# Attention scores on two half arrays of TensorE, even and odd heads side by side, six of nine products of parts, masks of 64 columns

## The reference

```python
q = (x @ Wq).reshape(bsz, seq_len, NH, HD).transpose(0, 2, 1, 3)
k = (x @ Wk).reshape(bsz, seq_len, KVH, HD).transpose(0, 2, 1, 3)
...
q = q * cos + rotate_half(q) * sin
k = k * cos + rotate_half(k) * sin
...
att = jnp.einsum('bhqd,bhkd->bhqk', q, k) * scale
att = jnp.where(causal, att, jnp.finfo(att.dtype).min)
att = jax.nn.softmax(att, axis=-1)
y = jnp.einsum('bhqk,bhkd->bhqd', att, v)
```

## Time and profile before

| | us |
|---|---|
| median of three runs | 1807.9 |
| the profiled execution | 1808.5 |
| its span, first to last instruction | 1806.8 |
| attention stage, from the first score product to the next stage | 232.4 to 855 |
| of it PE busy | 595.1 |
| of it DVE / ACT / POOL busy | 422.4 / 381.5 / 235.3 |
| PE clock granted in the stage | 0.96 of full speed |

### The profile page before, as it was taken

The page is one execution under the profiler, slowest core; times in us unless marked ns, Lnnn a source line. Parts: engine busy times, 40 slices in busy tenths (PEclk is TensorE's granted clock), DMA queues, the critical chain, the costliest instruction groups (busy, mean ns, idle before and its releaser), DMA issues. The chain is left out here.

```text
span 1806.8 us, 38981 instructions
## 1 busy us (share of the span) xinstructions
PE 1556.2 (86%) x11698; PEld 1092.2 (60%) x11698; DVE 1269.5 (70%) x3160; ACT 1156.7 (64%) x2439; POOL 771.7 (43%) x1202
## 2 busy tenths in 40 slices
PE   3999589999999999997799269999977834999998
PEld 1445245555555555553355159999964524999997
DVE  3787367777777777772786657787768766777776
ACT  3788316666666666665587347877847623788775
POOL 2587614334333444333343456655302203665540
PEclk9999759999999999998899579999989856999999
DMA  5022331111111111100011311111001100111110
GB/s 140 23 70 62 92 75 41 39 43 42 43 43 43 43 42 40 38 19 2 12 36 35 105 28 39 39 32 29 21 1 32 40 24 21 51 49 46 46 44 23
DMA packets 72828, 76.49 MB, mean 42 GB/s; under 512 B 13040, under 2 KB 61488, under 8 KB 72752
## 3 DMA queue, kind: packets, MB, share of 16 engines
q1 hardware_dynamic: 64560, 58.77, 11.2%
q0 software_dynamic: 8192, 16.79, 3.5%
HBM read 51.40 MB, written 24.12 MB: 42 GB/s over the span
## 5 line engine op out<-in xcount | busy, mean ns | idle before, releaser
L1024 DVE TENSOR_REDUCE at_negmax<-at_s_ps 128x2 f32<-128x1024 f32 (+3 forms) x384 | 393.2, 1045 | 170.3 <-PE at_s_ps L815 167.4
L936 ACT ACTIVATE at_p<-at_x_ps 128x512 f32<-128x512 f32 x640 | 353.5, 591 | 158.0 <-PE at_x_ps L825 151.2
L991 POOL TENSOR_SCALAR_AFFINE_SELECT at_p<-at_p 128x256 f32<-128x256 f32 (+1 forms) x448 | 190.8, 438 | 347.5 <-ACT at_p L936 347.5
L1248 POOL DMA_INDIRECT e_x_in<-xn,e_row_c x256 | 259.6, 1014 | 146.0 <-issue 85.0
L813 PE MATMUL at_s_ps<-at_kr,at_qr 72*128 72x512 bf16 (+3 forms) x1024 | 252.9, 312 | 23.2 <-DMA at_kr<-k_parts 20.7
L825 PE MATMUL at_x_ps<-at_qr,at_kr 74*128 74x512 bf16 (+3 forms) x1024 | 235.7, 305 | 22.6 <-ACT at_p L936 12.9
L1369 DVE TENSOR_TENSOR e_hid_lo<-e_hid,e_hid_hi 128x512 fp32r<-128x512 f32 x256 | 177.4, 694 | 83.2 <-ACT e_hid_hi L1333 74.5
L815 PE MATMUL at_s_ps<-maskb,identb 128*128 128x128 bf16 x1024 | 202.1, 225 | 0.0
L1332 ACT ACTIVATE e_hid<-e_h_ps 128x512 f32<-128x512 f32 x256 | 154.7, 604 | 42.1 <-PE e_h_ps L1274 37.4
L840 PE MATMUL at_o_ps<-at_p,at_va 128*32 128x512 f32 (+3 forms) x2048 | 155.5, 445 | 1.6 <-POOL at_p L991 1.6
L1274 PE MATMUL e_h_ps<-e_x_hi,w_hi 128*128 128x256 f32 x512 | 156.6, 306 | 0.0
(11 more groups left out here) (196 smaller groups left out, 3495.6 us busy)
## 6 DMA issues: line engine op xcount, KB each, us to landing
at_qr<-q_parts SPq DMA_DIRECT2D x192, 96.0 KB
k_parts<-m_kparts SPq DMA_DIRECT2D x48, 96.0 KB, 1.8
at_kr<-k_parts SPq DMA_DIRECT2D x64, 72.0 KB
xres<-in_x_dram SPq DMA_DIRECT2D x8, 512.0 KB, 7.6
xn<-m_n_xhat SPq DMA_DIRECT2D x16, 256.0 KB
e_x_in<-xn,e_row_c POOLq DMA_INDIRECT x256
xn<-sc_n_xhat SPq DMA_DIRECT2D x16, 256.0 KB
out_dram<-xres SPq DMA_DIRECT2D x16, 256.0 KB
```

The source lines that it names most:

```text
L936: a.activation(p_sb[g % 2][:, i, :], x_ps[i % 2][:], ACT.Exp, scale=SCALE).then_inc(x_read, 1)
L991: sel = gp.affine_select(out=part, in_=part, compare_op=ALU.is_ge, fill=0.0, base=0, pattern=[[0, n] for n in part.shape[1:-1]] + [[1, P]] ...
L1024: v.tensor_reduce(negmax[u][:, h0:h0 + len(heads), c], s_ps[k % 2][:, 0:len(heads) * pitch].rearrange("p (j w) -> p j w", w=pitch)[:, :, 0:w],
L1248: nc.gpsimd.indirect_dma_start(out=x_in[k][u][:], out_offset=None, in_=xn_dram, in_offset=bass.IndirectOffsetOnAxis(ap=row_c[k][:, u:u + 1 ...
```

## The change

The parts of q and k are paired six ways in place of nine: part 0 of k with parts 0, 1, 2 of q, part 1 with 0 and 1, part 2 with 0 (KEPT = 3, 2, 1), so KQ = 48 and KM = 50. The three smallest products of parts are left out. Partitions 0 to 63 now hold even heads and 64 to 127 odd heads, with the keys in both halves; qr shrinks to half its width. Score products of an even and an odd head are issued in pairs, one on the upper and one on the lower 64 rows of the array, into different banks. The mask, which had one product of 128 rows and 128 columns per head, has two of 64 rows and 64 columns per head (selb, maskb). The X tiles alternate between the halves (`i % 2`). max_rows moves from after X3 to after X2 and ahead of weigh, and ScalarE's copy of it from after the exponential of X4 to after that of X2. A group's loads are eight DMAs in place of four, and the maxima go to qr in two DMAs in place of one. One more constant of 256 columns is loaded and cast.

```diff
-KQ = PARTS * PARTS * HD
+KEPT = [PARTS - j for j in range(PARTS)]
+KFIRST = [sum(KEPT[:j]) for j in range(PARTS)]
+KQ = sum(KEPT) * HD
...
+HALF = P // 2
...
-        ("mhalf", W * C), ("wu", M * 4), ("wtop", M), ("maskf", P), ("gw", E), ("rowbase", 1),
+        ("mhalf", W * C), ("wu", M * 4), ("wtop", M), ("maskf", P), ("self", 2 * P), ("gw", E), ("rowbase", 1),
...
-        ("identb", [P, P], BF16), ("maskb", [P, P], BF16),
+        ("selb", [P, 2 * P], BF16), ("maskb", [P, P], BF16),
...
-                v.tensor_copy(h["identb"][:], h["ident"][:])
+                v.tensor_copy(h["selb"][:], h["self"][:])
...
-                            for copy in range(PARTS):
-                                sp.dma_start(k_dram[i * W + b].rearrange("(j c p) t -> c p j t", c=PARTS, p=KR)[copy],
-                                             rot["k"]["parts"][b * KR:(b + 1) * KR]).then_inc(parts_out[W], 16)
+                            rows = k_dram[i * W + b].rearrange("(x p) t -> p x t", p=KR)
+                            for j, copies in enumerate(KEPT):
+                                part = rot["k"]["parts"][b * KR:(b + 1) * KR, j, :]
+                                sp.dma_start(rows[:, KFIRST[j]:KFIRST[j] + copies, :],
+                                             part.unsqueeze(1).to_broadcast([KR, copies, T])).then_inc(parts_out[W], 16)
...
-          [[(2, 2 * i, 0), (2, 2 * i + 1, 256)] for i in range(GH // 2)]
+          [[(2, i, 0), (2, i + 2, 256)] for i in range(GH // 2)]
...
-S_TILES = [(3, (0, 1), 512), (3, (2, 3), 512), (2, (0, 1), 512), (2, (2, 3), 512), (1, (0, 1, 2, 3), 256), (0, (0, 1, 2, 3), 128)]
+S_TILES = [(3, (0, 1)), (3, (2, 3)), (2, (0, 1)), (2, (2, 3)), (1, (0, 1, 2, 3)), (0, (0, 1, 2, 3))]
...
-WEIGH_AT, ROWS_AT, MISC_AT = 2, 3, 7
+WEIGH_AT, MISC_AT = 2, 7
...
-        qr = [t(f"qr{u}", [P, NH * T], BF16) for u in range(2)]
+        qr = [t(f"qr{u}", [P, NH // 2 * T], BF16) for u in range(2)]
...
-                    q = q_dram[n].rearrange("(r h) t -> r h t", h=NH)
+                    q = q_dram[n].rearrange("(r g a s) t -> s g r a t", g=NKV, a=2, s=2)
...
-                    rows = PARTS * HD
-                    for j in range(PARTS):
-                        sp.dma_start(qr[u][j * rows:(j + 1) * rows, g * GH * T:(g + 1) * GH * T].rearrange("r (h t) -> r h t", h=GH),
-                                     q[:, g * GH:(g + 1) * GH, :]).then_inc(qk_in[u][g], 16)
-                    sp.dma_start(kr[u][0:KQ, g * T:(g + 1) * T], k[:, g, :]).then_inc(qk_in[u][g], 16)
+                    for half in range(2):
+                        for j, kept in enumerate(KEPT):
+                            at = half * HALF + KFIRST[j] * HD
+                            sp.dma_start(qr[u][at:at + kept * HD, g * 2 * T:(g + 1) * 2 * T].rearrange("r (a t) -> r a t", a=2),
+                                         q[half, g, 0:kept * HD]).then_inc(qk_in[u][g], 16)
+                        sp.dma_start(kr[u][half * HALF:half * HALF + KQ, g * T:(g + 1) * T], k[:, g, :]).then_inc(qk_in[u][g], 16)
...
-                    sp.dma_start(qr[u][KQ:KM, g * GH * T:(g + 1) * GH * T],
-                                 m_dram[u].rearrange("a r q -> a (r q)")[:, g * GH * T:(g + 1) * GH * T]).then_inc(m_in[u][g], 16)
+                    for half in range(2):
+                        sp.dma_start(qr[u][half * HALF + KQ:half * HALF + KM, g * 2 * T:(g + 1) * 2 * T].rearrange("a (x t) -> a x t", x=2),
+                                     m_dram[u].rearrange("a (g x s c) q -> s g a x (c q)", g=NKV, x=2, s=2)[half, g]).then_inc(m_in[u][g], 16)
...
-                def scores(n, u, r, g, k):
+                def scores(n, u, r, g, k, first):
...
-                        pe.wait_ge(qk_in[u][g], r * 64 + 64)
-                    c, heads, pitch = S_TILES[k]
+                        pe.wait_ge(qk_in[u][g], (r + 1) * 2 * (PARTS + 1) * 16)
+                    c, heads = S_TILES[k]
...
-                    for x, j in enumerate(heads):
-                        q0, at = (g * GH + j) * T + c * P, x * pitch
-                        pe.matmul(s_ps[k % 2][:, at:at + w], qr[u][0:KQ, q0:q0 + P], kr[u][0:KQ, g * T:g * T + w],
-                                  start=True, stop=False)
-                        mm = pe.matmul(s_ps[k % 2][:, at + w - P:at + w], h["identb"][:], h["maskb"][:], start=False, stop=True)
+                    for a in range(len(heads) // 2):
+
+                        pair = []
+                        for half in (first, 1 - first):
+                            rows = slice(half * HALF, half * HALF + KQ)
+                            q0 = (g * 2 + (heads[0] + 2 * a) // 2) * T + c * P
+                            pair.append((slice(half * HALF, (half + 1) * HALF), half * T + a * w))
+                            pe.matmul(s_ps[k % 2][:, half * T + a * w:half * T + (a + 1) * w], qr[u][rows, q0:q0 + P],
+                                      kr[u][rows, g * T:g * T + w], start=True, stop=False)
+                        for x in range(2):
+                            for rows, at in pair:
+                                at += w - P + x * HALF
+                                mm = pe.matmul(s_ps[k % 2][:, at:at + HALF], h["selb"][rows, x * P:(x + 1) * P],
+                                               h["maskb"][rows, x * HALF:(x + 1) * HALF], start=False, stop=x == 1)
...
-                        pe.wait_ge(m_in[u][g], r * 16 + 16)
+                        pe.wait_ge(m_in[u][g], (r + 1) * 2 * 16)
...
+                    rows = slice(i % 2 * HALF, i % 2 * HALF + KM)
...
-                        q0 = (g * GH + j) * T
-                        mm = pe.matmul(x_ps[i % 2][:, at:at + T - c * P], kr[u][0:KM, g * T + c * P:g * T + (c + 1) * P],
-                                       qr[u][0:KM, q0 + c * P:q0 + T], start=True, stop=True)
+                        q0 = (g * 2 + j // 2) * T
+                        mm = pe.matmul(x_ps[i % 2][:, at:at + T - c * P], kr[u][rows, g * T + c * P:g * T + (c + 1) * P],
+                                       qr[u][rows, q0 + c * P:q0 + T], start=True, stop=True)
...
-                                scores(*ahead, S_BEFORE[i])
+                                scores(*ahead, S_BEFORE[i], i % 2)
...
+                            if i == WEIGH_AT and ahead_rows is not None:
+                                max_rows(*ahead_rows, use(n, g, True))
...
-                            if i == ROWS_AT and ahead_rows is not None:
-                                max_rows(*ahead_rows, use(n, g, True))
...
-                            scores(*FIRST, g, k)
+                            scores(*FIRST, g, k, 0)
...
+                            if i == WEIGH_AT and ahead_rows is not None:
+                                copy_rows(ahead_rows[0], ahead_rows[3], use(n, g, True))
...
-                            if i == ROWS_AT + 1 and ahead_rows is not None:
-                                copy_rows(ahead_rows[0], ahead_rows[3], use(n, g, True))
...
-                    c, heads, pitch = S_TILES[k]
+                    c, heads = S_TILES[k]
...
-                    v.tensor_reduce(negmax[u][:, h0:h0 + len(heads), c],
-                                    s_ps[k % 2][:, 0:len(heads) * pitch].rearrange("p (j w) -> p j w", w=pitch)[:, :, 0:w],
-                                    AX.X, ALU.max, negate=True).then_inc(s_read, 1)
+                    scored = s_ps[k % 2][:].rearrange("p (s x) -> p s x", s=2)[:, :, 0:len(heads) // 2 * w]
+                    if len(heads) == 2:
+                        out = negmax[u][:, h0:h0 + 2, c]
+                    else:
+                        scored = scored.rearrange("p s (a w) -> p a s w", w=w)
+                        out = negmax[u][:, h0:h0 + GH, c].rearrange("p (a s) -> p a s", s=2)
+                    v.tensor_reduce(out, scored, AX.X, ALU.max, negate=True).then_inc(s_read, 1)
...
-        k_dram = dram("k_parts", [NB, PARTS * 96, T], BF16)
+        k_dram = dram("k_parts", [NB, KQ * NKV, T], BF16)
...
-    w["mask"] = np.where(at[None, :] > at[:, None], f32(MASKED), f32(0))
+    row, last = at % HALF, at % HALF == HALF - 1
+    later = np.where(row[:, None] < np.arange(HALF)[None, :], f32(MASKED), f32(0))
+    w["mask"] = np.concatenate([later, np.where(last[:, None], f32(MASKED), later)], 1)
+    same = (row[:, None] == np.arange(HALF)[None, :]).astype(f32)
+    none = np.zeros((P, HALF), f32)
+    w["self"] = np.concatenate([same, none, np.where(last[:, None], f32(1), none), np.where(last[:, None], f32(0), same)], 1)
```

## The result

The changed kernel takes 1810.35 us (median of 12 runs, 1808.26 to 1818.22), the kernel before 1808.15 in the same measurements (12 runs): a ratio of 1.0023, with a 95% interval of 1.0012 to 1.0034. That is no gain, at most 0.3% lost, where 1774 had been forecast. The profiled execution has a span of 1809.7 us against 1806.8.

A forecast was written before the change was run, and what follows sets the result against it. PE's instruction stream in the attention step was taken as the bound, with DVE and ACT not far behind. 1808.5 - 35.4 + 1 + 0.6 = 1774.7, set to 1774 us against the median; range 1748 to 1812.

The forecast's parts named there:

- What bounds the kernel: Attention stage: PE's stream sets the step, 35.74 of 36.98 us busy; DVE and ACT mostly wait for PE.
- The step: Attention steps with scores ahead: 0.6 us shorter each, 59 steps, 35.4 us in all (bounds 21 and 50).
- (a): Rival: short mask products are paced by their issue, four costing 0.23 us; steps 0.3 us longer, 1828 us; chance 0.08.
- (c): Rival: products on the two half arrays don't overlap here; 1808 to 1812 us, no change; chance 0.06.
- rival (d): X tiles on the other half overlap scores, misc passings free: 0.85 to 1 us a step, 1750; chance 0.08.
- max_rows: Row transpose in the attention step, now between X2 and weigh: keeps 0.11 us, its wait for the maxima adds nothing.
- The end of the stage: Last three attention steps: they have no scores and gain nothing.
- rival (b): PE's clock falls once in a step and returns with weigh: plus 24 + 2, 1834 us; chance 0.12.
- The start: Start of the attention stage, up to the first weigh: net plus 1 us, bounds minus 2 and plus 4.
- The 0.6 us for the constant of 256 columns: Constant adding 128 KB ahead of all compute: plus 0.6 us.

The follow-up runs named there:

- before_split: The kernel before with each mask product of 128 columns cut into two of 64, on the full array: 1838.5 us, ratio 1.0175.
- after_halfmask: The changed kernel with only the second of each head's two mask products, 16 instead of 32 a step: 1794.2 us, ratio 0.9932.
- before_six: The kernel before with six of nine products of parts, on the full array with 128-column masks, and nothing else: 2288.5 us, ratio 1.2656.

## Why the prediction was wrong

**What bounds the kernel** was read rightly: PE's stream in the step, with DVE and ACT waiting for it. Fewer masks, and the transpose taken off the way to weigh, shortened the step; idle products in PE's waiting for ACT did not lengthen it.

**The step** was right but for a small part. X5 comes 1.30 us after S2's start, X7 2.38 (forecast 1.30 and 2.37), X8 3.53, X2 5.68 and weigh 6.20 once the 0.5 us of project are taken off (3.48, 5.62, 6.1). The gain was 0.53 us and not 0.6, so 31 us in place of 35. Pairs ran side by side, and four masks took 0.06 us: rivals (a) and (c) did not come. That 1810 us lies where rival (c) had put the time is chance. X tiles on the other half did run beside score products, as rival (d) supposed (at 479.96 X1 and a product of S1 start 3 ns apart), but the step gained no more by it. The Trainium skill (TensorE: Matmul & The Clock Gate, Wait — 56ns, not 53.3ns?) gives about 62 ns for each matmul where hardware decoding is off; by an estimate from that figure four masks would take 0.25 us. The row from 500.91 to 500.97 decides against it here.

**max_rows** stood on the path between X2 and weigh at 0.11 us, and that was near: 0.48 us were forecast from X2 to weigh, 0.52 came. What had no term is the place that it left, behind weigh, where the waiting of X5 covered it. Put back there, in straight-line code, it saves 0.13 us a step.

**The code of the loop** is the step of the forecast that failed. The part on the change went through products, masks, loads and waits, and had no term for the fact that TensorE's loop grew from 1526 to 1782 recorded instructions. The five jumps, at no cost before, took 27.4 us: 17.1 of stops, and the rest in steps at a low clock behind them. before_split shows the stops without any half array, after_halfmask shows their absence with them. Nothing in the rows that I chose could price it, but the page's row of q8 and the times of its packets would have shown that the kernel before kept its loop loaded, which is the thing that could be lost.

**The end of the stage** was put down as no gain. It lost 5.9 us. Rows had it before them: the same steps brought the clock down once before (827.4 to 834.2). I took this as evidence on rival (b) within the steps and not on the place where it stood. That the clock falls was right in rival (b), but not where it put it: it fell at the jumps, in the two steps after the first weigh, and at the end, and in no other step of the loop.

**The start** was forecast 1 us later. The first weigh came 3.5 earlier. The loads began 1.3 us earlier than before and took 25.5 us, so the first maxima were stored at 252.35 and not 255; X began 3.4 us after that, where I had put 4.5; and from X0 to weigh it was 9.7 us, where I had 10.2. The two steps behind it gave 3.8 back. The 0.6 us for the constant of 256 columns had no row behind it and did not show: the stage began 1.3 us earlier than before.

That the last kernel stands at 1773.7 does not make the forecast right. It has no loop, merged masks, the transpose moved back and idle products: changes that the forecast did not speak of.

## What to carry to other kernels

Count the instructions of a loop on each engine before and after a change, and look whether the code queue is silent while the loop runs; if a change makes it speak in every pass, the jump has a price that no dependency shows. Here work was taken off the engine that is the bound, and its clock fell where it had not before; look for the stretches in which it now waits, and price them at the low clock, or fill exactly those. Fewer rows in a product are no gain by themselves: beside masks of 128 rows, products of 48 rows cost a passing each way, and the change avoided it by cutting both to halves.

## What the runs showed of the hardware

- A loop with 1526 recorded instructions on TensorE (1376 of them products and weight loads) stayed loaded, q8 silent behind the first pass, at both places tried. Loops of 1654 and 1782 (1504 and 1632 products and weight loads) did not, at any place tried. PE stood still 3.2 to 3.9 us at the jump, in two kernels once more for 1.3 to 2.8. With 256 of the 1782 being counter increments it did stay loaded. What exactly is counted, and how the place shapes the stop, is open.
- Straight-line code of over 11,000 TensorE instructions was fetched without a stop, by 64 to 72 packets in the whole kernel. The changed kernel's steps were 0.1 us longer in it than inside the loop; from 300 to 800 us X tiles waited 54.2 us for ACT in place of 42.1. Why was not settled.
- Passing from a product of 48 rows to one of 128 and back cost 0.1 us each way at the full clock; from 72 rows to 128 nothing that can be seen.
- In the changed kernel's steps the two products of S0, S2, S3 and S5 on two half arrays started 3 to 6 ns apart, and four masks of 64 columns on the halves took 0.06 us. In S4, and mostly in S1, the two started 0.14 to 0.22 us apart: one ran beside the X tile ahead, the other stood behind it on its half.
- The granted clock fell to 0.50 (1.2 GHz) after stretches with 2.5 of 3.4 us busy on half arrays, and stayed at 1.00 with the idle pair of 0.2 us added there. It was at 0.50 for much of the time while before_six was busy without a gap, with 48 to 50 rows and passings. A busy share alone does not tell what the clock will be. The Trainium skill (TensorE: Matmul & The Clock Gate, What's actually happening) has activity release the throttle of the clock; before_six, busy for 470 of 470 us at 0.65 on the mean, agrees with that no more than the 13.9 us of the earlier trace rows did.
